# Order of weight and row transfers at the start of two sorted expert layers, and new places for the tile lists and gates of the last one

## What is computed

```python
# L3f (L2f: gelu, biases, and a capacity per expert)
scores = softmax(h @ gate_w.T)
top_w, top_i = top_k(scores, 2); top_w /= top_w.sum(-1)
a = einsum('th,eih->eti', h, w1); g = einsum('th,eih->eti', h, w3)
eo = einsum('eti,ehi->eth', silu(a) * g, w2)
out = einsum('eth,te->th', eo, cw)      # cw: top_w at the two chosen experts
x = x + hidden_states + out
```

## Time and profile before

| | |
|---|---|
| median of 3 runs | 1133.97 us (1126.15 to 1136.29) |
| profiled execution | 1133.93 us, its span 1132.1 us |
| busy: TensorE, VectorE, ScalarE, GpSimd | 933.2, 681.2, 514.9, 495.0 us |
| mean granted TensorE clock | 0.902 of full |
| L2f's first pack issued, L3f's first pack issued | 667.38 us, 966.79 us |

### The profile page before, as it was taken

The page is one execution under the profiler, slowest core; times in us unless marked ns, Lnnn a source line. Parts: engine busy times, 40 slices in busy tenths (PEclk is TensorE's granted clock), DMA queues, the critical chain, the costliest instruction groups (busy, mean ns, idle before and its releaser), DMA issues. The chain is left out here.

```text
span 1132.1 us, 18158 instructions
## 1 busy us (share of the span) xinstructions
PE 933.2 (82%) x6440; PEld 738.9 (65%) x6440; DVE 681.2 (60%) x1708; ACT 514.9 (45%) x949; POOL 495.0 (44%) x480
## 2 busy tenths in 40 slices
PE   4888999999988999969898768799367874499992
PEld 3566788888877989834354337699145653488882
DVE  7876558999575343564564554444598764555443
ACT  1666544454445434324343424555255551355552
POOL 4445257788142101510012334457366555655552
PEclk9999999999997999977886967899689986599997
DMA  9999921111000000254532032564200001555543
GB/s 358 184 191 189 191 99 47 47 47 38 1 1 1 1 1 1 108 137 108 131 90 61 25 108 87 167 203 141 75 1 1 1 8 34 161 152 180 181 136 112
DMA packets 84272, 107.66 MB, mean 95 GB/s; under 512 B 7121, under 2 KB 62520, under 8 KB 83792
## 3 DMA queue, kind: packets, MB, share of 16 engines
q1 hardware_dynamic: 78040, 95.97, 34.3%
q0 software_dynamic: 4992, 8.45, 2.2%
q10 hardware_dynamic: 1152, 2.10, 0.5%
HBM read 68.71 MB, written 38.96 MB: 95 GB/s over the span
## 5 line engine op out<-in xcount | busy, mean ns | idle before, releaser
L3068 ACT ACTIVATE hT<-PS,par 128x512 f32<-128x512 f32 x200 | 136.6, 689 | 157.9 <-PE PS L2939 156.3
L1649 POOL TENSOR_TENSOR score<-score,mx 128x1232 f32<-128x1232 f32 x32 | 72.0, 2249 | 90.4 <-DVE mx L1520 90.4
L3147 DVE SCALAR_TENSOR_TENSOR X<-PS,wts,X 128x128 f32<-128x128 f32 x176 | 49.5, 344 | 86.6 <-PE PS L2958 86.6
L3197 POOL CAST h_upper<-hT 128x512 fp32r<-128x512 f32 x96 | 82.2, 890 | 43.4 <-ACT hT L3068 42.6
L2625 PE MATMUL PS<-q_up,halves 128*112 128x256 f32 (+1 forms) x276 | 86.3, 313 | 13.9 <-DVE hT L2758 10.1
L3099 DVE TENSOR_TENSOR h_lower<-hT,h_upper 128x512 fp32r<-128x512 f32 x96 | 88.8, 982 | 13.9 <-POOL h_upper L3197 13.9
L2937 PE MATMUL PS<-x_up,w_halves 128*128 128x512 f32 x200 | 85.3, 427 | 0.2 <-ACT hT L3068 0.2
L1144 DVE TENSOR_REDUCE score<-PS 128x8 f32<-128x616 f32 x64 | 49.9, 796 | 58.6 <-PE PS L1026 47.4
L2938 PE MATMUL PS<-x_low,w_halves 128*128 128x512 f32 x200 | 79.9, 400 | 0.0
L2626 PE MATMUL PS<-q_up,halves 128*112 128x256 f32 (+1 forms) x276 | 79.7, 289 | 0.0
L2939 PE MATMUL PS<-x_up,w_halves 128*128 128x512 f32 x200 | 79.7, 398 | 0.0
(11 more groups left out here) (383 smaller groups left out, 2378.4 us busy)
## 6 DMA issues: line engine op xcount, KB each, us to landing
regA<-L3f_w SPq DMA_DIRECT2D x23, 704.0 KB
regB<-L2f_w SPq DMA_DIRECT2D x23, 578.0 KB
L2f_sorted_x<-empty_row SPq DMA_DIRECT2D x8, 1161.0 KB, 20.9
L3f_sorted_x<-empty_row SPq DMA_DIRECT2D x8, 1161.0 KB, 19.6
qb<-gates_by_expert SPq DMA_DIRECT2D x24, 256.0 KB, 3.1
regA<-L0f_w SPq DMA_DIRECT2D x4, 768.0 KB, 16.3
regA<-L2f_sorted_x SPq DMA_DIRECT2D x23, 129.0 KB, 3.7
regB<-L3f_sorted_x SPq DMA_DIRECT2D x23, 129.0 KB, 4.0
```

What stands on the lines that cost most here:

```text
L1649: nc.gpsimd.tensor_tensor(score[:, u % 3, :, :], score[:, u % 3, :, :], mx[:, u % 3, :].unsqueeze(2).to_broadcast([P, H, K]), ALU.subtract)\
L3068: nc.scalar.activation(hT[:, n % 2, k, :], PS[:, i % 4, :], c["act"], bias=pc(f"{tag}_b1")[:, col:col + 1]).then_inc(h_ready.sem, 1)
L3197: nc.gpsimd.tensor_copy(h_upper[:, n % 2, k, :], hT[:, n % 2, k, :]).then_inc(h_up_ready.sem, 1)
```

## The change

On SyncE, in L2f and L3f: the packs of tiles 2 and 3 used to be issued ahead of the wait for `full_scattered` and of the rows of tiles 0 to 4; now they are issued behind these rows, as pack 4 already was.

On VectorE, in L3f alone: `full_table` moves from `late_vector` into the attention, right behind `place` of the early part. `tile_table` and `gates` move from `late_vector` into the tile loop, behind `multiply(2)` at i = 1. The two operations that read the counts out of PSUM stay ahead of the loop as `read_totals`, since the loop's products overwrite that bank. In L2f the order on VectorE stays as it was: `read_totals` and `tile_table` stand together at i = 1.

```diff
@@ vector_start
                     place(v, st, due("place", u), bank_of(("ranks", due("place", u))))
+                    if parts[due("place", u)][1] == EARLY:
+                        full_table(v, st)
@@ late_vector
-                full_table(v, st)
                 apply(v, st, late)
                 late_choose(v, st)
                 late_place(v, st)
-                tile_table(v, st)
-                gates(v, st)
+                read_totals(v, st)
@@
+            def read_totals(v, st):
+                v.wait_ge(totals_psum.sem, totals_psum.at(1))
+                total = PS[:, late_banks[3], 0:2 * E].rearrange("p (a e) -> p a e", a=2)
+                nc.vector.tensor_copy(counts[:, 4, 0:E], total[:, 0, :]).then_inc(v_step, st.one())
+                v.wait_ge(v_step, st.n)
+                nc.vector.tensor_tensor(counts[:, 0, 0:E], counts[:, 4, 0:E], total[:, 1, :], ALU.add).then_inc(v_step, st.one())
+                v.wait_ge(v_step, st.n)
@@ sync
                     load_places(2, full)
-                    for i in range(2, 4):
-                        load_pack(i)
                     sp.wait_ge(ro["full_scattered"].sem, ro["full_scattered"].at(16 * 2 * EARLY))
                     for i in range(full):
                         load_rows(i)
-                    for i in range(4, full):
+                    for i in range(2, full):
                         load_pack(i)
                     load_places(full, full + 2)
@@ vector, tile loop
-                    if late_inside and i == 1:
+                    if not gated and i == 1:
+                        ro["read_totals"](v, st)
                         ro["tile_table"](v, st)
                     if gated and i + 1 < TILES:
                         multiply(i + 1)
+                    if gated and i == 1:
+                        ro["tile_table"](v, st)
+                        ro["gates"](v, st)
```

More of the change, by code:

```diff
@@ L2392, in full_table, with tile_table @@
                 v.wait_ge(v_step, st.n)
-            def tile_table(v, st):
+            def read_totals(v, st):
                 v.wait_ge(totals_psum.sem, totals_psum.at(1))
                 total = PS[:, late_banks[3], 0:2 * E].rearrange("p (a e) -> p a e", a=2)
-                n_rows, n_tiles, gap, start = counts[:, 0, 0:E], counts[:, 1, 0:E], counts[:, 2, 0:E], counts[:, 3, :]
                 nc.vector.tensor_copy(counts[:, 4, 0:E], total[:, 0, :]).then_inc(v_step, st.one())
                 v.wait_ge(v_step, st.n)
-                nc.vector.tensor_tensor(n_rows, counts[:, 4, 0:E], total[:, 1, :], ALU.add).then_inc(v_step, st.one())
+                nc.vector.tensor_tensor(counts[:, 0, 0:E], counts[:, 4, 0:E], total[:, 1, :], ALU.add).then_inc(v_step, st.one())
                 v.wait_ge(v_step, st.n)
+            def tile_table(v, st):
+                n_rows, n_tiles, gap, start = counts[:, 0, 0:E], counts[:, 1, 0:E], counts[:, 2, 0:E], counts[:, 3, :]
                 pairs = compared[:, 0:E * E].rearrange("p (e k) -> p e k", e=E)
@@ L2460, in sparse_route @@
                         late_turned=lambda a: rows_turned(a, late, late_banks[0]), late_copied=lambda a: rows_copied(a, late), scalar_gates=scalar_gates,
-                        late_choose=late_choose, late_place=late_place, tile_table=tile_table, gates=gates,
+                        late_choose=late_choose, late_place=late_place, read_totals=read_totals, tile_table=tile_table, gates=gates,
                         late_power=lambda p: pool_power(p, late), late_scatter=late_scatter,
```

## The result

The changed kernel takes 1139.41 us (median of 17 runs, 1134.53 to 1145.69), the kernel before, run beside it, 1133.68 us (17 runs). The ratio is 1.0058, 95% interval 1.0038 to 1.0078: 0.6% slower, some 6.6 us. The profiled execution took 1140.09 us with a span of 1138.3, so 6.2 above that of before. The forecast was 1134.5, +0.55. The time lies within the range given, but a loss of 6 us where 0.55 was forecast needs its cause.

A forecast was written before the change was run, and what follows sets the result against it. In the tile loops TensorE was taken as the busy engine, going round with ScalarE and VectorE, so only the heads and first tiles count. L2f -0.65 and L3f +1.2 gave +0.55 on 1133.93: 1134.5 us, range 1128 to 1141.

The forecast's parts named there:

- L3f's head: Before L3f's tile loop: rows 0 land 1.0 us sooner, VectorE is freed, and the first product starts 2.4 us sooner.
- The list: tile_table inside L3f's loop on VectorE, behind multiply(2): costs 3.1 us, bound 3.7 if blocked again beside GpSimd.
- The queue from the end of multiply(2) to pack 5's landing: L3f: list 3.15, SyncE up to the issue 3.6, transfer 3.9, together 10.65 us; ScalarE wants the pack after 7.1.
- 3.55: L3f: us by which pack 5 comes later than ScalarE wants it, paid whatever the head gives; net +1.15.
- the head's lead: L3f: 2.4 us gained before the loop, carried through the first tiles so that multiply(2) ends at 996.55, not 998.94.
- the late chain: L3f: full_table's new place starts the normalised rows 1.7 us later, at 966.9, and VectorE reaches the totals at 977.85.
- the -0.65: L2f: the first transpose no longer waits 0.88 us for tile 0's rows; gain 0.65 us, bounds 0 and 0.88.
- the stall at tile 4 is longer: Rival, chance 0.10: L3f's gap idles TensorE, its clock drops to half, a tile costs some 3 us more; 1138 to 1141.
- The head gives nothing: Rival, chance 0.20: L3f's first product starts no sooner, pack 5's 3.55 us stand alone; 1136.8.
- The likeliest case: The forecast itself, chance 0.40: L2f gains 0.65 us, L3f loses 1.2, so 1134.5 us.

The follow-up runs named there:

- full_table back: Changed kernel with full_table of L3f returned to the head of late_vector, ahead of apply; 1112.89 us, 0.9989 of the kernel before.
- six scatters in a row: Kernel before with SyncE's new order, full_table's last five operations behind the normalised rows, two of L3f's eight late scatters behind GpSimd's tile 2 weight half; 1128.83 us, 0.9985.
- the order alone: Kernel before with only SyncE's order changed, packs 2 and 3 behind the rows in both layers; 0.9999 and, again, 0.9984 of the kernel before.
- the places alone: Changed kernel with SyncE's old order, so only VectorE's order in L3f differs from the kernel before; 1140.01 us, 1.0062 of it.
- one scatter: Changed kernel issuing one of L3f's eight late scatters, the other seven blocks' rows missing from the sorted array; 1.0042 and, again, 1.0040 of the kernel before.

## Why the prediction was wrong by 5 us

**What held.** L3f's head came as worked out: normalised rows at 966.82 (forecast 966.9), rows 0 issued at 975.89 (975.8) and landed at 978.26 (978.3), first lower half at 979.81 (979.5). The list took 3.1 us and collided with nothing, SyncE issued rows 5 2.23 us behind it (2.3) and pack 5 1.14 behind these (1.2), and ScalarE waited for the pack (1.49, forecast 1.8). The runs with the list a tile sooner and later show that this queue is a cause. That the whole time fell into the range, with the mechanism of 4.8 of the 6.3 us right, owes something to the range's width: its upper end of 1141 came from a rival that did not happen.

**The term that was mis-sized.** The queue from the end of multiply(2) to pack 5's landing was to take 10.65 us against 7.1. It took 11.89: the pack needed 5.41 us, not 3.9. Rows 5 and 6 and packs 5 and 6 now go out together (both packs within one row of 2.14 us; before, that row took 5.86), so they share the DMA engines; that this alone made it 5.41 isn't shown, for where they go out in the same way the pack took 4.1 with full_table back, 4.8 with the list one tile later and 5.1 in the changed kernel's second profile. Beside it TensorE waited 1.76 for rows 5, which were taken at 2.5, the shortest of their layer, and needed 4.1. So 4.8 us instead of 3.55, 4.45 in the other profile of this kernel.

**The step that failed.** "`multiply(2)` ends at 998.94, so now at 996.55": the head's lead was carried through tiles 0 to 2. It ended at 1000.46, 3.9 later. The lead was real and was lost in tile 1, where ScalarE and TensorE stood still while GpSimd issued late scatters. These are tied to `row_at` and not to the first lower half, and the prediction had itself worked out that the late chain comes 1.7 us later; it charged that to the totals alone, not to the late scatters. Shown: the stall is in the trace of the changed kernel in one batch and not in another, with a loss of 0.58% and of 0.17%. Supported by one pair of profiles that differ in the tail too: with six scatters in a row instead of eight it was gone. Not shown: that the scatters cause the stall, and that the 1.75 us of full_table make up the later multiply(2) (+1.52), since the run that undid them met a batch without the stall. So this step failed, and what held up tile 1 stays open.

**L2f.** The first transpose no longer waits for rows and output(0) even came 2.7 us sooner. Before and after, output(0) and a later transpose; in the second fence also output(2):

```profile
692.43 1.95 PE L2637 MATMUL PS<-regB,hT 128*128 128x128 f32 x16
...
717.69 0.41 PE L2610 MATMUL PS<-par,regA 128*128 128x128 f32 x2 [1.93 <-DVE q_up L2744]
```

```profile
689.73 1.95 PE L2636 MATMUL PS<-regB,hT 128*128 128x128 f32 x16
...
704.87 3.79 PE L2636 MATMUL PS<-regB,hT 128*128 128x128 f32 x16 [8.14 <-DVE regA L2802]
...
717.41 0.41 PE L2609 MATMUL PS<-par,regA 128*128 128x128 f32 x2 [1.93 <-DVE q_up L2743]
```

Of the 2.7 us 0.28 were left at 717.4, and none at `row_at` of L3f's early part (959.10 and 959.08). The same kind of stall, 8.14 us on TensorE beside the late scatters of L2f and the output scatters behind them, took the rest. Before has it too: VectorE waits 7.72 us there, up to 708.95, and 7.39 in the changed kernel. In these profiles the -0.65 was 0. The two runs of the order alone (0.9999, 0.9984) agree, but their intervals reach some 3 to 4 us to either side and can't tell 0.65 from 0.

**The sum, again.** 4.8 from the list, 1.5 from multiply(2), 0 from L2f: 6.3, against 6.2 in the profiles. Of the rivals, "the stall at tile 4 is longer" has the measured time in its span (1138 to 1141), by luck: its mechanism did not come in the changed kernel, where output(3) took 1.95. It did come with the places alone, with full_table back and with one scatter: 3.32, 3.15 and 3.62 us for an output step behind a gap of 2.6, 2.4 and 3.2 us. "The head gives nothing" (1136.8) is nearer in kind, since the lead was lost, but it wanted a first lower half at 981.5 or later, and that stood at 979.81. The likeliest case was 5 us off because it summed leads and delays on the path and took for granted that nothing else holds up tiles 0 to 2.

## What to carry to other kernels

A lead at the head of a pipelined loop is worth something only if nothing later in the loop's first iterations is tied to another chain of work: before carrying it on, look for the work that is released by another chain (here eight scatters behind `row_at`) and ask when that ends. Work that produces addresses for a transfer must be costed together with the whole burst behind it: a list two tiles ahead of its use looked nearly free, but from the end of multiply(2) to the landing of its pack it was 11.9 us, where 7.1 were to be had. And repeat a result of half a per cent in another batch: the loss was 0.6% in one and 0.2% in the other, with overlapping intervals, and what the traces differ in was a stall of its own.

## What the runs showed of the hardware

The same kernel before takes 1131 to 1134 us in some batches and 1114 in others. In the changed kernel, profiled in both, the first pack of L2f is issued at 667.52 and 662.73, and the first of L3f at 964.30 and 945.18, so the difference is collected in places over the second half. Between 640 and 980 us it shows as idle time that the profile puts down to "remote" or "issue", in part beside rows of indirect scatters (38.9 us on ScalarE and VectorE in the first profile, none in the second, counting waits above 0.5 us). The record gives the same chip number, 3, for the first batch and the third, in which before took 1132.57 and 1114.13 us, so a chip's number doesn't tell which it will be; the mechanism is open.

VectorE and GpSimd hold each other up: VectorE's 0.62 us weight half took 2.08 beside GpSimd's, and with the list a tile later the list's first operation took 1.23 us instead of 0.22:

```profile
1005.58 1.16 POOL L2831 TENSOR_TENSOR halves<-regA,halves 128x448 fp32r<-128x448 f32 x1
...
1005.60 1.23 DVE L2405 TENSOR_TENSOR compared<-counts,par 128x64 f32<-128x64 f32 x1
```

The Trainium skill ("SBUF — State Buffer", section Terms) has the two arbitrate for one port pair, with the loser fully blocked; the trace agrees, VectorE's operation ending 0.09 us behind GpSimd's. In the one-scatter kernel VectorE's operation ended 0.48 us behind GpSimd's, though by the profile it had begun 0.45 us ahead of it.

Rows 5 landed late in both profiles of the changed kernel (TensorE waited 1.76 and 1.75 us) and not in that with full_table back, whose list was as late. The DMA view of the 3 us behind the issue has one difference. The changed kernel in its two profiles, 1007 to 1010 and 982.4 to 985.4:

```profile
q1 hardware_dynamic: 597, 0.71, 90.7%
q8 instruction: 1, 0.02, 2.1%
```

```profile
q1 hardware_dynamic: 630, 0.80, 87.8%
q8 instruction: 1, 0.02, 2.0%
```

With full_table back, 981.9 to 984.9:

```profile
q1 hardware_dynamic: 630, 0.82, 95.8%
```

(queue, packets, MB, share of the 16 engines). The trace's signals of the landing show fifteen of the sixteen parts of rows 5 in place by 1008.26 and the last at 1009.87 (983.55 and 985.33 in the second profile). One fetch of instructions on one DMA engine is the likely cause of 1.6 to 1.8 us for a transfer that is spread over all of them, and those waited on that part. The other two kernels whose rows 5 and 6 and packs 5 and 6 go out together have no fetch while rows 5 are under way, and these landed 2.4 us (places alone) and 2.3 us (list one tile later) after their issue, as with full_table back (2.3). It was not tried on purpose, and in the kernel before the row transfers of L3f take 4.0 us at the median, most of them issued right behind a pack, so a fetch is not the only thing that can make one late.
